# The front of a fused adaLN, fast-weight attention and MoE block: load order, first products and second modulation rearranged

## The reference, cut to what matters

```python
mod = (_silu(L0_c) @ L0_wmod).reshape(L0_c.shape[0], 6, 1, -1)
sa, ca, ga, sb, cb, gb = (mod[:, 0], mod[:, 1], mod[:, 2], mod[:, 3], mod[:, 4], mod[:, 5])
ga = (2 * (ga >= 0) - 1) * jnp.maximum(jnp.abs(ga), 0.25)
gb = (2 * (gb >= 0) - 1) * jnp.maximum(jnp.abs(gb), 0.25)
h = _layernorm(x, axis=-1) * (1 + ca) + sa
x = x + ga * _L0_attn_ref(h, ...)
h = _layernorm(x, axis=-1) * (1 + cb) + sb
x = x + gb * _L0_ffn_ref(h, ...)
```

## Time and profile before

| | us |
|---|---|
| median of three runs (lowest, highest) | 698.15 (696.43, 698.57) |
| the profiled execution's own time | 700.72 |
| its span, first to last instruction | 698.9 |

### The profile page before, as it was taken

One profiled execution on the slowest core, in us unless ns is written; L12 is line 12 of the kernel. 1 busy time (PEld: TensorE's weight loads), 2 busy tenths in 40 slices (PEclk: granted clock), 3 DMA queues, 4 the chain that ended last, 5 costly groups with the idle time before them and its releaser, 6 DMA issues.

```text
span 698.9 us, 11474 instructions
## 1 busy us (share of the span) xinstructions
PE 658.4 (94%) x4116; PEld 563.8 (81%) x4116; DVE 478.5 (68%) x949; ACT 336.3 (48%) x703; POOL 222.0 (32%) x210
## 2 busy tenths in 40 slices
PE   3989789799997899989999999999999999999997
PEld 3878689699986788878888888888888888888885
DVE  4598877989997778695446654676665666556545
ACT  3277689889995875633223223222322332232232
POOL 2276677887064862053001330033100330000000
PEclk9999999999999999999999999999999999999999
DMA  8120000120000000133003332133322432222223
GB/s 321 45 78 1 2 1 1 46 52 21 2 4 0 1 1 1 27 106 95 31 26 84 112 103 76 60 106 106 98 61 83 120 107 60 71 66 61 61 82 115
DMA packets 22568, 43.58 MB, mean 62 GB/s; under 512 B 3400, under 2 KB 5712, under 8 KB 22384
## 3 DMA queue, kind: packets, MB, share of 16 engines
q1 hardware_dynamic: 21488, 39.76, 19.1%
q10 hardware_dynamic: 832, 2.43, 0.9%
q0 software_dynamic: 192, 0.66, 0.2%
HBM read 40.60 MB, written 2.24 MB: 61 GB/s over the span
## 4 chain that ended last, share of the span: by engine, by line
PE 77%; DVE 10%; ACT 5%; POOL 3%; DMA 2%; issue 2%; ACTq 0%; DVEq 0%; SPq 0%
PE ps L1050 37%; PE ps L1127 18%; PE ps L860 3%; PE ps L897 2%; PE ps L975 2%; PE ps L964 2%; PE ps L988 2%; PE ps L989 2%; PE ps L1004 2%; DMA qkvw<-in_qkvw 1%; PE ps L1093 1%; DVE x L1517 1%; PE ps L1073 1%; PE ps L835 1%; ACT junk L637 1%
## 5 line engine op out<-in xcount | busy, mean ns | idle before, releaser
L770 ACT ACTIVATE sgm<-ps,zero 128x512 f32<-128x512 f32 x100 | 68.9, 690 | 269.8 <-PE ps L1050 269.7
L1568 DVE TENSOR_TENSOR am<-sgm,ps 128x512 f32<-128x512 f32 x88 | 60.6, 689 | 140.9 <-ACT sgm L770 140.8
L1050 PE MATMUL ps<-h2hi,whi 128*128 128x512 f32 x400 | 156.7, 392 | 0.0
L1050 PE MATMUL ps<-h2hi,wlo 128*128 128x512 f32 x400 | 156.0, 390 | 0.0
L1050 PE MATMUL ps<-h2lo,whi 128*128 128x512 f32 x400 | 155.9, 390 | 0.0
L481 POOL CAST whi<-raw 128x768 fp32r<-128x768 f32 x25 | 22.9, 914 | 238.4 <-DMA raw<-in_moew 238.2
L1050 PEld LDWEIGHTS ps<-h2lo,whi 128*128 128x128 f32 x400 | 75.3, 188 | 15.9
L1050 PEld LDWEIGHTS ps<-h2hi,whi 128*128 128x128 f32 x400 | 75.4, 188 | 15.5
L1050 PEld LDWEIGHTS ps<-h2hi,wlo 128*128 128x128 f32 x400 | 75.4, 188 | 15.4
L1127 PE MATMUL ps<-ahi,whi 128*128 128x512 f32 x200 | 77.9, 390 | 0.1
L1127 PE MATMUL ps<-ahi,wlo 128*128 128x512 f32 x200 | 77.8, 389 | 0.0
(11 more groups left out here) (211 smaller groups left out, 1220.2 us busy)
## 6 DMA issues: line engine op xcount, KB each, us to landing
raw<-in_moew SPq DMA_DIRECT2D x25, 384.0 KB, 3.9
cw<-combine SPq DMA_DIRECT2D x32, 256.0 KB, 3.3
cw<-combine SPq DMA_DIRECT2D x16, 224.0 KB, 3.0
cw<-combine SPq DMA_DIRECT2D x16, 192.0 KB, 2.8
cw<-combine SPq DMA_DIRECT2D x16, 160.0 KB, 2.7
wog<-combine SPq DMA_DIRECT2D x2, 1024.0 KB, 6.7
cw<-combine SPq DMA_DIRECT2D x16, 128.0 KB, 2.9
out<-x1T SPq DMA_DIRECT2D x8, 256.0 KB, 2.9
```

The costliest lines, as they stand in the source:

```text
L770: ac.activation(sgm[:, n % 2, :], gate_bank(n), ACT.Silu, bias=zero[:, :]).then_inc(S["e_sg"], 1)
L1050: last = mm(o, w_, a_[:, kc, tok], start=(kc == 0 and k == 0), stop=(kc == KC - 1 and k == 2))
L1568: ve.tensor_tensor(am[:, n % 2, :], sgm[:, n % 2, :], lin_bank(n), ALU.mult).then_inc(S["e_a"], 1)
```

## The change

- **Loads.** All but `wmod`'s shift and scale columns and the identity now go through SyncE's queue, in the order `cT`, `x` tiles 0-1, tiles 2-3, `qkvw` in two halves, `x` 4-7, `x` 8-15, the attention weights, `wnat`, `woT`, `onw`, and the other four parts of `wmod` last.
- **Statistics.** Blocks of 2, 2, 4, 4, 4 tiles.
- **Weights rounded by GpSimd**, half by half; `qkvlo` half by half on VectorE.
- **Products by part.** hi x hi for all halves and banks, then lo x hi, then hi x lo; only the second part waits for `h1lo`.
- **Second modulation** and the row `ga` after the last tile, copied out by ScalarE, gates formed by GpSimd.
- **Small work** from VectorE to ScalarE: the modulation out of PSUM, the converted and scaled identities, `woT`.
- **Warming products.** 11 products of `ones` by `ones` ahead of the modulation and 4 ahead of the first tile; nothing reads them.

```diff
@@ sync
+            sp.dma_start(x[:, 0:2, :], x_d[:, 0:2, :]).then_inc(S["ld_x0"], 16)
+            sp.dma_start(x[:, 2:4, :], x_d[:, 2:4, :]).then_inc(S["ld_xa"], 16)
+            for c in range(KC):
+                sp.dma_start(qkvw[:, c, :], qkvw_d[:, c, :]).then_inc(S[f"ld_qkv{c}"], 16)
...
+            sp.dma_start(wnat[:, :, :], wnat_d).then_inc(S["ld_wn"], 16)
+            sp.dma_start(woT[:, :, :], wo_d).then_inc(S["ld_wn"], 16)
+            sp.dma_start(onw[:, :], onw_d).then_inc(S["ld_wn"], 16)
+            sp.dma_start(wmod2[:, :, :], wmod_d[:, :, 2 * D:]).then_inc(S["ld_mod2"], 16)
...
-            sp.wait_ge(S["ga_ok"], 4)
+            sp.wait_ge(S["ga_ok"], 5)
@@ gpsimd
+            inverse_deviation(0)
+            inverse_deviation(1)
+            for c in range(KC):
+                po.wait_ge(S[f"ld_qkv{c}"], 16)
+                po.tensor_copy(qkvhi[:, c, :], qkvw[:, c, :]).then_inc(S["qw_hi"], 1)
+            h1_low(0)
...
+            def gate_of(dst, mag, sign, done, base):
+
+                po.tensor_scalar(sign, dst, 0.0, 2.0, ALU.is_ge, ALU.mult).then_inc(done, 1)
+                po.wait_ge(done, base + 1)
+                po.tensor_scalar(sign, sign, -1.0, None, ALU.add).then_inc(done, 1)
+                po.wait_ge(done, base + 2)
+                po.tensor_tensor(mag, sign, dst, ALU.mult).then_inc(done, 1)
+                po.wait_ge(done, base + 3)
+                po.tensor_scalar(mag, mag, 0.25, None, ALU.max).then_inc(done, 1)
+                po.wait_ge(done, base + 4)
+                po.tensor_tensor(dst, sign, mag, ALU.mult).then_inc(done, 1)
+
             gate_slope(0)
+            po.wait_ge(S["mod2_sb"], 1)
+            po.tensor_scalar(modc[:, CB, :, :], modc[:, CB, :, :], 1.0, None, ALU.add).then_inc(S["mod2_ok"], 1)
+            gate_of(modc[:, GB, :, :], gab[:, :, :], gsg[:, :, :], S["mod2_ok"], 1)
+            po.wait_ge(S["ga_sb"], 1)
+            gate_of(garow[:, :], gaab[:, :], gasg[:, :], S["ga_ok"], 0)
             po.wait_ge(S["lr_ok"], 1)
             po.wait_ge(S["sc_k"], NT)
             key_rates(0)
@@ scalar
+            ac.wait_ge(S["mod_ps"], 1)
+            ac.activation(modc[:, SA, :, :], psum_mod[:, SA, :, :], ACT.Copy).then_inc(S["mod_ok"], 1)
+            ac.activation(modc[:, CA, :, :], psum_mod[:, CA, :, :], ACT.Identity, bias=ones[:, 0:1]).then_inc(S["mod_ok"], 1)
...
+                if t == 0:
+                    ac.wait_ge(S["ld_id"], 16)
+                    ac.activation(identb[:, :], ident[:, :], ACT.Copy).then_inc(S["ident_ok"], 1)
+                    for k in range(NS_STEPS):
+                        ac.activation(aI[:, k, :], ident[:, :], ACT.Copy, scale=NS[k][0]).then_inc(S["ident_ok"], 1)
...
+                if t == NT + 2:
+                    ac.wait_ge(S["mod_ps"], 2)
+                    ac.activation(modc[:, SB_:GB + 1, :, :], psum_mod2, ACT.Copy).then_inc(S["mod2_sb"], 1)
                 if i in (2, 3) and blk >= 1:
                     turned_out(blk - 1, i - 2)
+                if t == NT + 3:
+                    ac.wait_ge(S["ga_ps"], 1)
+                    ac.activation(garow[:, :], bank(6)[0:B, 0:D], ACT.Copy).then_inc(S["ga_sb"], 1)
+                if t == 14:
+                    ac.activation(woT[:, :, :], woT[:, :, :], ACT.Copy, scale=onw[:, 0:1]).then_inc(S["wo_ok"], 1)
@@ tensor
+            def spin(count):
+
+                for _ in range(count):
+                    mm(bank(7)[:, 0:P], ones[:, :], ones[:, :], start=True, stop=True)
...
+            pe_.wait_ge(S["const"], 3)
+            spin(11)
             pe_.wait_ge(S["silu_c"], 1)
             pe_.wait_ge(S["ld_mod"], 16)
...
+                if t == 0:
+                    spin(4)
...
-                    pe_.wait_ge(S["h1_lo"], b + 1)
-                    pe_.wait_ge(S["qw_lo"], 1)
+                    pe_.wait_ge(S["h1_hi"], b + 1)
+                    for k, (h_, w_) in enumerate(((h1hi, qkvhi), (h1lo, qkvhi), (h1hi, qkvlo))):
+                        if k == 1:
+                            pe_.wait_ge(S["h1_lo"], b + 1)
                         for c in range(KC):
+                            if t == 0 and k != 1:
+                                pe_.wait_ge(S["qw_hi" if k == 0 else "qw_lo"], c + 1)
+                            for o, n0, n1 in ((bank(4 + t % 2), 0, BLK), (bank(6 + t % 2), BLK, QKV + NLR)):
+                                last = mm(o[:, 0:n1 - n0], h_[:, b % 2, c, tok], w_[:, c, n0:n1], start=(c == 0 and k == 0), stop=(c == KC - 1 and k == 2))
...
-                if t == 0:
+                if t == NT + 1:
                     pe_.wait_ge(S["ld_mod2"], 16)
-                    pe_.wait_ge(S["mod_sb"], 1)
-                    modulation((SB_, CB, GB))
+                    pe_.wait_ge(S["v_sb"], 2 * NT)
+                    modulation((SB_, CB, GB), bank(7), wmod2, GA)
                 if t == NT:
                     fast_up(0)
                 if i in (2, 3) and blk >= 1:
                     turned(blk - 1, i - 2)
+                if t == NT + 2:
+                    for kc in range(KC):
+                        last = mm(bank(6)[0:B, 0:D], scT[:, kc, :], wmod2[:, kc, 0:D], start=(kc == 0), stop=(kc == KC - 1))
+                    last.then_inc(S["ga_ps"], 1)
@@ vector
+            STATS = ((0, 2), (2, 4), (4, 8), (8, 12), (12, 16))
...
-            ve.wait_ge(S["qw_hi"], 1)
-            ve.tensor_tensor(qkvlo[:, :, :], qkvw[:, :, :], qkvhi[:, :, :].bitcast(F32), ALU.subtract).then_inc(S["qw_lo"], 1)
+            for c in range(KC):
+                ve.wait_ge(S["qw_hi"], c + 1)
+                ve.tensor_tensor(qkvlo[:, c, :], qkvw[:, c, :], qkvhi[:, c, :].bitcast(F32), ALU.subtract).then_inc(S["qw_lo"], 1)
```

More of the change, by code:

```diff
@@ L139, in carve @@
             return made, where
-        (wmod, xn, sq, garow, gaab, gasg, wnat), end = carve(R_tmp, [
-            ("wmod", [P, KC, 6 * D], F32), ("xn", [P, 4, D], F32), ("sq", [P, 2, BLK], F32),
-            ("garow", [B, D], F32), ("gaab", [B, D], F32), ("gasg", [B, D], F32), ("wnat", [P, 6, P], F32)])
+        (wmod, xn, sq, wnat), end = carve(R_tmp, [
+            ("wmod", [P, KC, 2 * D], F32), ("xn", [P, 4, D], F32), ("sq", [P, 2, BLK], F32), ("wnat", [P, 6, P], F32)])
         assert end <= R_wo
+        (wmod2, garow, gaab, gasg), end = carve(R_wo, [
+            ("wmod2", [P, KC, 4 * D], F32), ("garow", [B, D], F32), ("gaab", [B, D], F32), ("gasg", [B, D], F32)])
+        assert end <= R_wo + B * NH * D * 4
         (h1hi, h1lo, qkvw, qkvhi), end = carve(R_dw, [
@@ L257, in build, with stats_of @@
         WIDE = 4
+        STATS = ((0, 2), (2, 4), (4, 8), (8, 12), (12, 16))
+        def stats_of(b):
+            return [k for k, (t0, t1) in enumerate(STATS) if t0 <= b * TPB < t1][0]
         def scaled(b):
@@ L396, in h1_low @@
                 po.tensor_tensor(h1lo[:, b % 2, :, :], h1T[:, b % 2, :, :], h1hi[:, b % 2, :, :].bitcast(F32), ALU.subtract).then_inc(S["h1_lo"], 1)
-            for b in range(4):
+            inverse_deviation(0)
[4 more added lines that the diff above has]
+            h1_low(0)
+            for b in range(1, 4):
                 if b < 3:
-                    inverse_deviation(b)
+                    inverse_deviation(b + 1)
                 h1_low(b)
@@ L778, in _, with modulation @@
             mm = pe_.matmul
-            def modulation(js):
+            def modulation(js, out, w, j0):
                 for j in js:
@@ L784, in modulation @@
                         for kc in range(KC):
-                            last = mm(bank(3)[:, (j * KC + c) * B:(j * KC + c + 1) * B],
-                                      wmod[:, kc, j * D + c * P:j * D + (c + 1) * P], scT[:, kc, :], start=(kc == 0), stop=(kc == KC - 1))
+                            last = mm(out[:, (j * KC + c) * B:(j * KC + c + 1) * B],
+                                      w[:, kc, (j - j0) * D + c * P:(j - j0) * D + (c + 1) * P], scT[:, kc, :], start=(kc == 0), stop=(kc == KC - 1))
                 last.then_inc(S["mod_ps"], 1)
+            def spin(count):
+                for _ in range(count):
+                    mm(bank(7)[:, 0:P], ones[:, :], ones[:, :], start=True, stop=True)
             def xn_turned(b):
@@ L838, in fast_up @@
                 last.then_inc(S["up_ps"], 1)
+            pe_.wait_ge(S["const"], 3)
+            spin(11)
             pe_.wait_ge(S["silu_c"], 1)
             pe_.wait_ge(S["ld_mod"], 16)
-            modulation((SA, CA))
+            modulation((SA, CA), bank(3), wmod, 0)
             pe_.wait_ge(S["ld_id"], 16)
@@ L891, in grads @@
                     pe_.wait_ge(S["dw_sb"], NH * b)
+                else:
+                    pe_.wait_ge(S["mod2_sb"], 1)
+                    pe_.wait_ge(S["ga_sb"], 1)
                 for h in range(NH):
@@ L1160, in _, with stats @@
             ve.memset(mone[:, :], -1.0).then_inc(S["const"], 1)
-            def stats(blk):
-                for t in range(blk * 4, blk * 4 + 4):
+            def stats(k):
```

(10 more changed lines are left out.)

83 lines of the change are left out of this document (20 added, 63 removed).

## The result

The changed kernel took 688.81 us, the median of four runs (686.80 to 692.47), against 698.36 for the kernel before (four runs, 696.43 to 699.79): a ratio of 0.9885, with a 95% interval of 0.985 to 0.9919. The profiled execution took 688.01, its span 686.1. A second series of eight runs gave 689.15 against 696.52 (17 runs), 0.9903 (0.9865 to 0.994). The change makes the kernel faster by 7.4 to 9.6 us. One run of the first series and three of the second (692.47 to 694.73) stand at a lower mean granted clock, 0.977 to 0.980, than the others, 0.985 to 0.993; all are counted. The gain was put too large by a third or more.

What follows compares the result with a forecast made beforehand. The front was bound by a chain of waits, the projection by TensorE with VectorE close behind, the passage not by TensorE. The terms -12.6 - 1.0 + 0.8 = -12.8 took 698.15 to 685.4 us, range 681.5 to 690.

Steps and rivals of the forecast that it cites:

- the passage: From fast_up(0) at 73.19 into the gradients: gates on GpSimd ahead of the key rates lose 0.8 us.
- The gates' own price: GpSimd's gate steps ahead of the key rates: 5.0 us together, where GpSimd idled 4.35; one-input steps 0.47 each.
- a gate step on GpSimd over 1 us: Sign that the forecast is wrong, in GpSimd's gates ahead of the key rates.
- T1: End of tile 1's products in the front: from 30.59 to 18.0 us, a gain of 12.6 (9.7 to 15.5).
- At no cost: VectorE's 4.8 us chain of rates may end up to 0.6 later, hidden under GpSimd's lateness.
- The projection: From T1 to the passage, 42.6 us before: VectorE reaches the first sums earlier, 1.0 us off (none to 1.5).
- The move of the second modulation: Its narrow matmuls and ga leave TensorE's order ahead of tile 1: 6.7 us of the gain at T1.
- the second rival: Gates on GpSimd and VectorE's chain of rates run one behind the other: lr 4.8 late, 689.4 us; chance 0.13.
- the third: Rival in the front: the clock stays low through tile 1, T1 20.9, 688.3 us; chance 0.10.
- The early warming raises the clock before the modulation: Rival in the front: T1 15.1, 682.5 us; chance 0.12.
- A comparison costs like a power: Rival on GpSimd's three one-input steps on ga: a comparison or maximum takes 45 us, total 730; chance 0.03.
- VectorE holds the projection: Rival: the front is quicker but VectorE's pace, busy 38.89 of 42.2 us, holds the projection; 698 us, chance 0.02.

Runs made afterwards that it cites:

- second trace: The changed kernel run again with no edit and profiled a second time; 689.15 us, ratio 0.9903.
- gates late: Against the changed kernel, GpSimd's eleven gate steps moved behind the gradients, ahead of the splitting of the expert weights; 686.41 us, ratio 0.985.
- warm passage: The changed kernel plus 16 products of ones between fast_up(1) and grads(0), gates not moved; 688.12 us, ratio 0.9871.
- no second warming: The changed kernel without the four warming products ahead of tile 0; 688.54 us, ratio 0.9888.
- the second trace of the kernel before: The kernel before, unedited, run once more for a second profile; 698.35 us, span 696.5.
- late gates, no second warming: The kernel of gates late, without the four warming products ahead of tile 0; 686.37 us, ratio 0.985.
- rounding on ScalarE: The changed kernel with the weights rounded half by half on ScalarE instead of GpSimd; 689.80 us, ratio 0.9894.

## Why the prediction was right in direction and wrong in size

**The step that failed is the passage: "I take 0.8 lost".** Between `fast_up(0)` and the last product of the gradients the lead shrank by 4.0 (13.2 to 9.2). GpSimd, which set the path, explains 2.6 of it, and the clock 1.5 (2.8 and 1.5 in the second trace):

- *The gates' own price, 1.4 more than forecast.* "The three with one input lie between 0.24 and 0.65; I take 0.47, by the cast's slope." They take 1.08, 0.94 and 0.84, 2.86 in sum instead of 1.41, and 2.76 with no chain of rates beside them. The upper end of the bound was itself too low: on this shape a step with one input is dearer than a two-input one (0.72), and a cast says nothing about a comparison, an addition or a maximum. So 6.4 us stood in a gap of 4.35, not 5.0: 2.05 late instead of 0.65. Two of the prediction's own signs of being wrong came: "a gate step on GpSimd over 1 us" (1.08), and holes of TensorE after T1 of more than 3 us (the largest alone has 4.03).
- *Their start, 0.5.* GpSimd comes to the gates 10.5 us after `fast_up(0)` (59.98 to 70.48), where before it fell idle after 9.9 (83.13, which is 87.48 less its 4.35). The passage did not make this. GpSimd's scaling of the last block, ahead of the gates, started 12.65 earlier than before, released by VectorE both times, while TensorE reached `fast_up(0)` 13.2 earlier: the other engines followed the quicker projection by half a microsecond less. In gates late GpSimd waits for `lr`; there it is VectorE's chain that starts 9.9 us after `fast_up(0)` instead of 9.3, and that separates its passage from that of before (17.3 to 16.7).
- *The chain of rates, nothing.* It has 14 steps, not 15, and was stretched from 4.88 to 5.49, but `lr` stood ready 1.58 before GpSimd was free. "At no cost" was right.
- *The clock, 1.5.* Not in the sum at all. The sum had priced when `grads(0)` starts and not how fast it runs: behind the longer hole (4.03 us) the granted clock is lower and 24 products take 4.41 instead of 2.92. In the one trace of warm passage the fall does not come. It came in four of five traces with that hole open; what else decides it stays open.

The rows of GpSimd on which the second point rests, before and after:

```profile
70.17 3.14 POOL L411 TENSOR_TENSOR qk<-qk,rn 128x256 f32<-128x256 f32 x4 [1.00 <-DVE rn L1203]
```

```profile
57.52 3.13 POOL L428 TENSOR_TENSOR qk<-qk,rn 128x256 f32<-128x256 f32 x4 [0.99 <-DVE rn L1257]
```

With 4.0 for 0.8 the forecast would have been a gain of 9.6, or 688.6 from its own base.

**The base was a second, smaller error.** The kernel before ran at 696.26 to 696.67 in the three later sittings, below the 698.15 of three runs; and the profiled execution carried a hole and a fall of the clock near 312 us that a second one did not have there. So its 12.8 to the changed kernel's trace hold 3.6 that came behind the last product of the gradients, where the change does nothing; the 7.8 and 9.2 at that product agree with the 7.4 and 9.6 of the medians.

**What was right.** T1: 18.27 for 18.0, though through two errors that cancel in this trace and not in the second (19.35): the first product late by 1.25, with the warming products at 0.39 us each instead of 0.21 behind a late second normalisation, and the clock high earlier. With equal sharing, `wmod` came at 5.89 (6.1 forecast). The DMA view of 0 to 60 us, in slices of 1.5 us, shows why `x` did not follow at 4.6:

```profile
GB/s 0 63 337 331 393 420 442 395 397 373 407 178 11 0 5 0 0 0 0 0 5 0 0 0 0 0 0 11 0 0 0 0 0 0 0 0 0 0 0 0
```

By 6.0 us 1.10 MB have moved ((63 + 337 + 331) x 1.5 us), when only `wmod` (0.52) and `x` 0-1 (0.26) were complete: about 0.3 MB belonged to transfers issued behind them (the identity, 0.07 MB, can be among them). A transfer that is issued later moves bytes before the earlier ones are complete, and takes its share from them. The projection: T1 to `fast_up(0)` took 41.7 us instead of 42.6, 0.9 for a forecast 1.0. The move of the second modulation: 5.3 at T1 and 5.2 to 5.8 in the times, instead of 6.7, and nothing lost by it in the passage. What the loads, the smaller blocks and the products by part share of the other 7 us at T1 no run tells.

**The rivals.** The measured 688.8 lies near the price of the second rival (689.4) and the third (688.3), but neither mechanism carried it. *Gates and rates exclude each other* asked for 4.8 us more; 0.6 came in all, and even that lay under GpSimd's own lateness. The lock that the prediction takes from the Trainium skill (SBUF — State Buffer, "Who interferes with whom") shows in the last step of the rates (0.69 for 0.27), which ended when GpSimd's two-input product beside it did (74.46 to 75.18), and in the normalisation beside the cast (1.73 for 0.73). But the sentence quoted there, on a VectorE instruction with two SBUF inputs, is not borne out by the rest of the chain: it ran beside the gates nearly throughout, and six two-input steps beside GpSimd's one-input steps on `ga` took 1.92 us instead of 1.72. There the measurement decides. *The clock stays low through tile 1* did not happen: tile 1 took 2.12 us. *The early warming raises the clock before the modulation* happened in part: in eight of the nine traces with the early group the modulation took 1.85 to 2.23 us (in the ninth, of no second warming, 3.56), and in the three without that group 3.55 to 3.56. It did not stay: TensorE then waited for `xn`, and in the changed kernel's first trace the granted clock is 0.50 from 9 to 14 us, under the transposes and the four warming products. So it gained nothing at T1. *A comparison costs like a power*: 1.08 us, refuted. *VectorE holds the projection*: refuted by the 0.9.

## What to carry to other kernels

When work is moved from an engine that is busy to one that is idle, price it by rows of the same operation and shape on the new engine, and where there is none, let the bound go well past the nearest row: here three steps at twice their price stood in front of everything. Put the moved work where its result is first needed, not where its input is first ready; moving the gates behind the gradients gave the two fastest versions of this study (686.4, below both kernels). And when a hole of TensorE grows, ask what the products behind it cost at the low clock: here 1.5 us, in four of five traces.

## What was not expected of the hardware

**At the same number of elements, a row of 8 partitions is dearer on GpSimd.** 256 columns on 8 partitions take 0.72 to 1.08 us, 16 columns on 128 partitions 0.22 to 0.29, though the second has as many elements (2048). And on 8 partitions the steps with one input (0.84 to 1.08) are dearer than those with two (0.72).

**When the first products start says little about when they end.** In the second trace of the kernel before, the first product starts at 19.55 us instead of 16.65 and T1 is the same, 30.57. In the changed kernel and its variants with the modulation moved, first products at 12.0 to 13.8 give a T1 of 18.1 to 19.4 in no order: 12.0 with 19.20 (late gates, no second warming), 12.64 with 18.07 (rounding on ScalarE), 13.75 with 18.27 (after). The three earliest (11.97 to 12.46) are those without the four warming products, and their first tiles run longer at the low level.
